# Moving the first two residual loads, one bias add and one weight split within the opening of a fused attention and FFN kernel

## The reference, cut to what matters

```python
xn = _layernorm(x)                      # x: (8, 1024, 256) f32
qkv = xn @ qkv_w + qkv_b                # 16 heads of 16
q, k = _l2norm(q), _l2norm(k)
kv = einsum('bhnd,bhne->bhde', k, v)    # per batch and head
attn = einsum('bhnd,bhde->bhne', q, kv) @ proj_w + proj_b
ffn = relu(xn @ W1 + b1) @ W2 + b2      # 256 -> 1024 -> 256
out = x + attn + ffn
```

## Time and profile before

| what | value |
| --- | --- |
| median of 3 runs | 584.23 us (584.19 to 585.92) |
| the profiled execution: its own time | 584.19 us |
| its span, first to last instruction | 582.5 us |
| PE busy | 571.3 us, 98% |
| DVE, ACT, POOL busy | 426.2, 264.5, 101.7 us |
| mean granted TensorE clock | 0.997 |
| DMA, mean over the span | 77 GB/s |

### The profile page before, as it was taken

The page is one execution under the profiler, slowest core; times in us unless marked ns, Lnnn a source line. Parts: engine busy times, 40 slices in busy tenths (PEclk is TensorE's granted clock), DMA queues, the critical chain, the costliest instruction groups (busy, mean ns, idle before and its releaser), DMA issues.

```text
span 582.5 us, 10386 instructions
## 1 busy us (share of the span) xinstructions
PE 571.3 (98%) x3624; PEld 518.4 (89%) x3624; DVE 426.2 (73%) x803; ACT 264.5 (45%) x486; POOL 101.7 (17%) x103
## 2 busy tenths in 40 slices
PE   7999799999999999999999999999999999999997
PEld 6788699989899998999999989998989989899897
DVE  5895778768776778768788587776977677873653
ACT  3673462544625454264532555345363454523421
POOL 1337140030302103030210303003030120300300
PEclk9999899999999999999999999999999999999999
DMA  8221231250323313141312503125032231213011
GB/s 290 96 103 38 43 82 58 69 150 20 86 78 81 100 32 77 76 142 34 74 34 88 153 16 83 43 76 153 16 84 79 44 102 27 45 72 107 3 36 73
DMA packets 79739, 44.60 MB, mean 77 GB/s; under 512 B 70116, under 2 KB 72932, under 8 KB 79720
## 3 DMA queue, kind: packets, MB, share of 16 engines
q1 hardware_dynamic: 79712, 44.34, 27.1%
q10 hardware_dynamic: 8, 0.01, 0.0%
HBM read 20.20 MB, written 8.39 MB: 49 GB/s over the span
## 4 chain that ended last, share of the span: by engine, by line
PE 84%; DVE 6%; ACT 4%; SPq 3%; issue 1%; DMA 1%; POOL 1%; DVEq 0%; POOLq 0%
PE o_bank L895 11%; PE o_bank L896 11%; PE o_bank L894 10%; PE w_bank L894 9%; PE w_bank L895 9%; PE w_bank L896 9%; PE v_bank L894 6%; PE v_bank L895 6%; PE v_bank L896 5%; SPq L271 3%; PE g_bank L894 3%; PE g_bank L895 3%; PE g_bank L896 3%; DVE qT_lo L598 1%; ACT h_hi L470 1%
## 5 line engine op out<-in xcount | busy, mean ns | idle before, releaser
L894 PE MATMUL o_bank<-w_hi,h_hi 128*128 128x256 f32 x512 | 144.7, 283 | 1.2 <-DVE y_sb L760 1.2
L895 PE MATMUL o_bank<-w_lo,h_hi 128*128 128x256 f32 x512 | 145.1, 283 | 0.0
L896 PE MATMUL o_bank<-w_hi,h_lo 128*128 128x256 f32 x512 | 144.9, 283 | 0.0
L470 ACT ACTIVATE h_hi<-w_bank 128x512 fp32r<-128x512 f32 x128 | 76.5, 597 | 129.4 <-PE w_bank L896 127.5
L732 DVE SCALAR_TENSOR_TENSOR h_lo<-w_bank,h_hi 128x512 fp32r<-128x512 f32 x128 | 87.4, 683 | 35.3 <-ACT h_hi L470 32.7
L331 POOL TENSOR_TENSOR xn_lo<-xn,xn_hi 128x256 fp32r<-128x256 f32 x60 | 44.5, 741 | 377.3 <-ACT xn_hi L407 373.8
L894 PEld LDWEIGHTS o_bank<-w_hi,h_hi 128*128 128x128 f32 x512 | 100.5, 196 | 7.1 <-DVE h_lo L732 1.6
L895 PEld LDWEIGHTS o_bank<-w_lo,h_hi 128*128 128x128 f32 x512 | 100.4, 196 | 4.5
L894 PE MATMUL w_bank<-xT_hi,w_hi 128*128 128x512 f32 x254 | 101.0, 398 | 2.1 <-DVE h_lo L732 2.0
L896 PEld LDWEIGHTS o_bank<-w_hi,h_lo 128*128 128x128 f32 x512 | 100.5, 196 | 0.0
L895 PE MATMUL w_bank<-xT_lo,w_hi 128*128 128x512 f32 x254 | 100.4, 395 | 0.0
(11 more groups left out here) (142 smaller groups left out, 976.3 us busy)
## 6 DMA issues: line engine op xcount, KB each, us to landing
y_sb<-x SPq DMA_DIRECT2D x16, 512.0 KB, 4.4
qT_lo<-blocks SPq DMA_DIRECT2D x256, 32.0 KB, 1.9
x_sb<-x SPq DMA_DIRECT2D x15, 512.0 KB, 4.3
xT_raw<-blocks SPq DMA_DIRECT2D x224, 32.0 KB, 1.9
out<-y_sb SPq DMA_DIRECT2D x14, 512.0 KB, 2.6
y_sb<-w SPq DMA_DIRECT2D x4, 256.0 KB, 4.9
out<-y_sb SPq DMA_DIRECT2D x4, 256.0 KB, 2.0
w_raw<-w SPq DMA_DIRECT2D x1, 768.0 KB, 8.8
```

Source lines behind the costliest of these rows:

```text
L470: nc.scalar.activation(h_hi[:, j % RING, :], w_bank[j % 2][:], ACT.Relu).then_inc(h_done, 1)
L894: nc.tensor.matmul(to, left[0], right[0], start=first, stop=False, skip_group_check=shared)
L895: nc.tensor.matmul(to, left[0], right[1], start=False, stop=False, skip_group_check=shared)
L896: return nc.tensor.matmul(to, left[1], right[0], start=False, stop=last, skip_group_check=shared)
```

## The change

Three things move within `opening`; nothing is added or taken away.

1. SP: the two `load_y` of batch 0 are issued behind `load_x(4, 0)`, the wait for POOL and PE, and the 16 transfers of `move_x(2)`, and ahead of `move_q(0, 0)`.
2. POOL: `add_bias(0, 0)` with its waits stands behind the split of the projection weights instead of ahead of it.
3. DVE: `w1_low(3)` stands ahead of the `wqk_lo` subtraction instead of behind it.

```diff
             def opening():
-                load_y(0, 0)
-                load_y(0, 1)
                 load_x(4, 0)
                 sp.wait_ge(xn_split_done, 2 * TILES)
                 sp.wait_ge(xT_ready, 2 * KC)
                 move_x(2)
+                load_y(0, 0)
+                load_y(0, 1)
                 move_q(0, 0)
...
                 nc.gpsimd.tensor_tensor(bias_out[:], bias_out[:], bias_ffn, ALU.add).then_inc(bias_out_ready, 1)
-                pool.wait_ge(bias_out_ready, 1)
-                add_bias(0, 0)
                 pool.wait_ge(wvp_loaded, 32)
                 nc.gpsimd.tensor_copy(proj_hi[:], proj_raw).then_inc(wvp_hi_ready, 1)
                 pool.wait_ge(wvp_hi_ready, 1)
                 nc.gpsimd.tensor_tensor(proj_lo[:], proj_raw, proj_hi[:].bitcast(F32),
                                         ALU.subtract).then_inc(wvp_ready, 1)
+                pool.wait_ge(bias_out_ready, 1)
+                add_bias(0, 0)
                 split_xn(2, 0)
...
                 h_low(0, 3)
+                w1_low(3)
                 dve.wait_ge(wqk_hi_ready, 1)
                 less(wqk_lo[:], wqk_raw, wqk_hi[:]).then_inc(wqk_ready, 1)
-                w1_low(3)
```

## The result

The changed kernel takes 587.61 us (median of 6 runs, 587.44 to 590.45) against 584.51 us (median of 6 runs, 584.19 to 585.92) for the kernel before in the same comparison: a ratio of 1.0063, with a 95% interval of 1.0042 to 1.0084. The profiled execution took 587.35 us with a span of 585.6 us, 3.16 us more than that of before. It is slower, at the place and by the chain that were named, and by a little less than was forecast (588.3 us).

The account below looks back on a forecast made before the run. PE, busy 98% of the span, sets the time through gather's start. DVE's 74.3 us plus 1.6 us of POOL contention gave 75.9 us, later than PE's 74.7: +4.1 on 584.19 gives 588.3 us, range 586.3 to 590.4.

Parts of the forecast that it names:

- The change is worth what it does to the moment at which PE starts gather.: PE has no gap from gather(1, 0, 1) at 71.78 us onward, so a delay there reaches the end whole.
- The loads go out when the 16 transfers are out, at 56.97 us.: On SP, move_x(2) still starts at 46.54 us and takes 10.38 us; the bias loads issue next.
- 3.47 us until POOL can use the load: Load issue to POOL's add_bias, taken from batch 1, giving 60.44 us; the other bound was 5.6 us.
- `add_bias`, `add_ffn`, PE's return.: add_bias takes 2.40 us, DVE's add_ffn follows near 62.9 us, PE starts ffn_down at 63.7 us, 5.8 us later.
- DVE's side: DVE needs 6.45 us from add_ffn to h_low(1, 2); with 1.6 us of POOL contention it allows gather at 75.9 us.
- From `h_low(1, 2)` to `gather` 4.96 us: On DVE, the present 6.23 us less the 1.27 us wait for move_q(0, 0), giving 74.3 us before POOL contention.
- PE's side: From 63.7 us PE does 6.31 us of work, loses 1.67 us at half clock, then 2.96 us: gather at 74.7 us.
- Edit 2 nothing by itself, and a saving beside late loads: POOL's projection-weight split runs while POOL would await the load, costing nothing; left behind, it would lengthen POOL's work beside DVE.
- Edit 3 "absorbed: 0 on the path; 0.6 us if the chain of the moves turns out to hang on PE": w1_low(3) first delays PE's first query_key by 0.5 to 0.7 us, absorbed in PE's wait for add_ffn.
- the low end of the forecast, 586.7 us: Case where DVE meets no POOL and PE's 74.3 to 74.7 us decides gather.
- the one in which the stalls give everything back: Rival: shrinking PE stalls and an unrepeated half-clock price leave +1.2 us, 585.4 us, with gather before 73.5 us; 8%.
- The costly one: Rival: a second half-clock stretch on PE (590.0 us) or the first load taking 5.6 us (590.4 us); 23%.

Follow-up runs that it names:

- e1_loads_only: Kernel before with only the two y_sb loads moved behind move_x(2), POOL and DVE orders as before: median 591.54 us, ratio 1.0079.
- e12_loads_pool: Kernel before with the late loads and POOL's add_bias behind the projection-weight split, without the w1_low(3) move: median 590.10 us, ratio 1.0063.
- w_warm: Changed kernel with 26 unused identity products on PE ahead of ffn_down(1, 0, 1, 0), filling its wait: median 588.08 us, ratio 1.0054 to the kernel before.
- p_split_first: Changed kernel with POOL's split_xn(2, 0) ahead of the waiting add_bias(0, 0): median 587.95 us, ratio 1.0046 to the kernel before.
- e3_split_only: Kernel before with only w1_low(3) moved ahead of wqk_lo on DVE: median 583.50 us, ratio 0.9972.
- e2_pool_only: Kernel before with only POOL's add_bias(0, 0) moved behind the split of the projection weights, loads early: median 585.53 us, ratio 0.9991.
- k_swap: Kernel before with DVE's sum_squares(1, 0) placed ahead of k_low(0, 0): median 585.77 us, ratio 1.0009.
- k_late: Kernel before with DVE waiting for ACT's k_hi, then doing sum_squares(1, 0), then k_low(0, 0): median 583.06 us, ratio 0.9967.

## Why the prediction was right, and where it was off

The forecast was +4.1 us at `gather` and 588.3 us; measured were +3.20 us and 587.35 us in the profiled execution. By its own steps, with the moments of the traces as they stand:

- **"The change is worth what it does to the moment at which PE starts gather."** Right: 507.13 us follow, against 507.17 us (counted to the start of PE's last product, 71.78 to 578.95 us) in before, and 506.96 to 507.18 us in all others but two. In those two, the half clock fell into the gather itself (508.3 us, last section).
- **The loads go out when the 16 transfers are out, at 56.97 us.** The rule was right, the time 1.21 us too late: 55.76 us. It rested on the sentence that the transfers "start at 46.54 us because they wait for POOL's `split_xn(1, 1)`", which is true, and on leaving the length of that split as it was. Of the 1.21 us, 1.04 us are the split and the rest is after's earlier start.
- **3.47 us until POOL can use the load**, from batch 1: 3.95 us, 0.48 us too little; in e1_loads_only, e12_loads_pool and w_warm it was 3.82 to 3.86 us. Between the bounds of 3.47 and 5.6 us the nearer row was a good choice.
- **`add_bias`, `add_ffn`, PE's return.** 2.34 us for 2.40; DVE at 62.15 for 62.9 us, PE at 62.99 for 63.7 us, all by the difference above. PE stood idle for 5.84 us and not for 7.0 us, because it came back 0.7 us earlier and had arrived about 0.4 us later (in e12_loads_pool, without edit 3, it was 7.37 us).
- **DVE's side 6.45 us to `h_low(1, 2)` plus 1.6 us of POOL.** The two together are 7.83 us instead of 8.05 us; POOL's part is 1.47 us by rows, and p_split_first gave the same 1.5 us back. A middle value between 0 and 3.3 us was taken because two meetings of 0.5 and 1.1 us fit; there were three (0.13, 0.55 and 0.79 us). That the sum came so near is in part luck.
- **From `h_low(1, 2)` to `gather` 4.96 us**: 5.00 us. The wait for `move_q` was indeed covered.
- **PE's side.** The slow stretch was priced at 1.67 us, from the only one in the trace, and cost 2.1 us, by the comparison with w_warm. Length times lost clock, 5.28 us x 0.50 = 2.64 us, would be too much. From its return to `gather` PE needed 11.12 us where the forecast had 6.31 + 1.67 + 2.96 = 10.94 us. The longer stretch cost nothing, since PE's side was not the later one: PE still waited 0.87 us for `k_low(1, 1)`, and w_warm took the whole stretch away for no gain.
- **Edit 2 nothing by itself, and a saving beside late loads**: 0.03 us and 1.20 us, right both times.
- **Edit 3 "absorbed: 0 on the path; 0.6 us if the chain of the moves turns out to hang on PE".** This is the term that was mis-sized, and it explains the miss: it measured -0.92 us (e12_loads_pool against after) and -0.90 us (e3_split_only against before). The chain of the moves did hang on PE's 0.6 us, by way of ACT and `k_low(0, 0)`, with the other sign: later on DVE meant first for POOL. The stretched fourth subtraction, 1.79 us beside three of 0.74 us, was in the trace of before, and the same rule had been used for the other end of the change; it was not asked of the step that edit 3 shifts.
- **Three readings that did no harm.** "No wait on PE is for POOL now" overlooks the 2.3 us for `ident` at the start of the kernel, which no edit touches. And the low end of the forecast, 586.7 us, takes DVE's 74.3 us although PE's 74.7 us would then be the later side: by the forecast's own rule it is 587.1 us. And of the two stretched rows that are said to agree with the rule for two SBUF inputs, only the add of 4 columns is such a case; `bound` reads one tile.

With edit 3 left out the forecast of +4.1 us stands against +4.30 us measured in e12_loads_pool. So 75.9 us - 1.21 (earlier moves) + 0.48 (load) - 0.06 (`add_bias`) - 0.22 (DVE) + 0.04 = 74.93 us, against 74.98 us. Apart from the earlier moves the terms add up to 0.24 us because 0.48 us and 0.28 us have different signs.

Of the rivals, the one in which the stalls give everything back needed `gather` before 73.5 us; it didn't come about, since DVE's work without any wait fills the time. The costly one had a half of its condition come true: the half clock lasted twice as long as before. It came out dearer only in those runs whose mean clock was 0.991, 589.82 and 590.45 us; it wasn't profiled in one of them, so where in the kernel their clock fell stays open. (A third dear run, 589.37 us at 0.994, fits a late start.)

## What to carry to other kernels

A load that has slack in front of a queue isn't free to move behind a batch of small transfers: what counts is the issue time of the whole batch (16 x 0.65 us here) plus its own landing, against the wait that it was covering. When an edit delays an engine by a few tenths, look for the pairs of operations of DVE and POOL that begin within those tenths of each other, and for who waits on the stretched one; a stretched row in a group whose others are short marks such a pair. Before paying for a slow clock, take away its cause with filler work for one run: if the stalls grow by what was won, another engine sets the time.

## What the runs showed of the hardware

**Two starts.** The profiles begin in one of two ways, about 2 us apart: `h_low(0, 3)` is at 23.8 to 24.2 us in eight of them and at 25.65 to 26.34 us in six. The timeline of PE's first rows in before and then in e3_split_only, which do the same there:

```profile
2.26 3.70 PE L1036 MATMUL w_bank<-ident 128*128 128x128 f32 x18 [2.26 <-POOL ident L354]
...
6.51 1.60 PE L1036 MATMUL w_bank<-ident 128*128 128x128 f32 x12
```

```profile
2.26 4.21 PE L1036 MATMUL w_bank<-ident 128*128 128x128 f32 x18 [2.26 <-POOL ident L354]
...
7.55 2.93 PE L1036 MATMUL w_bank<-ident 128*128 128x128 f32 x12
```

The second twelve products take 2.93 instead of 1.60 us, nearly half the pace, while the view by stages gives a granted clock of 1.00 for both stretches. So the granted clock doesn't show the difference in these first microseconds; the lengths of PE's products do. Whether the clock or something else makes them longer, and what decides between the two starts, is open. It costs the median up to 2 us, as much as most edits here.

**Where the half clock falls.** In before it fell 0.4 us behind the end of the 2.0 us stall, in after within the one of 5.8 us (at 61.45 us). In before it lasted from 66.65 to 70.06 us, ahead of a wait for DVE, which hid it. In the profiles of e2_pool_only and k_swap it came one stall later, inside the gather (stages of e2_pool_only):

```profile
74.00:76.00 2.00, 1.79 (x9) 1.82 (x10) 1.93 (x11) 0.00 (x0) 0.00 (x0) 0.57 0.26 56
76.00:78.00 2.00, 2.00 (x12) 2.00 (x12) 1.86 (x8) 0.20 (x1) 0.00 (x0) 0.58 0.22 45
```

In the gather it is whole in the time: from `gather` to the end 508.3 us instead of 507.1 us. Most runs of the kernel before gather near 584.2, 585.3, 586.05 and 587.1 us; two starts, each with and without such a 1.1 us, would fit that. The traces of k_swap (585.14 us, early start) and e2_pool_only (587.80 us, late start), whose `gather` starts as in before, are of this kind; of the dearer runs of before itself none was traced. One run at 583.31 us (mean clock 1.000) and four from 586.83 to 588.06 us (0.994) stay unexplained. k_late, with a mean clock of 1.000 in its profile, had no slow stretch at all behind the same stall of 2.00 us. The same idle time was thus followed by a slow stretch in one execution and by none in another.

**Hundredths decide a meeting.** In k_swap POOL's subtraction came 0.02 us behind DVE's `k_low` and took 1.79 us; in k_late it came 0.6 us ahead and took 0.74 us.
